# Products that nothing reads in thin half sub-steps of two attention passes, and new places for some VectorE work

## The reference, cut to what matters

```python
def _L1_attn_ref(x, Wq, Wk, Wv, Wo, bo):      # 16 heads of 16
    q, k, v = heads(x @ Wq), heads(x @ Wk), heads(x @ Wv)
    weights = softmax(q @ k.T / 4)
    return (weights @ v) @ Wo + bo
def _L1_ffn_ref(x, ...):                      # 8 experts of 32, the two best, low-rank part of 16
    w = top two of softmax(x @ G), zero elsewhere
    return sum_e w_e * down_e(silu(gate_e x) * up_e x) + sum_e w_e * B_e (A_e x)
x = layernorm(x + L1_attn(x)); x = layernorm(x + L1_ffn(x))
```

## Time and profile before

| | |
|---|---|
| median of 3 runs | 745.18 us |
| profiled execution: own time | 748.4 us |
| profiled execution: span of its instructions | 746.5 us |
| TensorE products busy | 702.6 us (94%) |
| VectorE, ScalarE, GpSimd busy | 508.2, 403.3, 106.0 us |
| first turned score of pass 0, 1, 2, 3 | 372.98, 449.69, 540.61, 624.46 us |

### The profile page before, as it was taken

The page is one execution under the profiler, slowest core; times in us unless marked ns, Lnnn a source line. Parts: engine busy times, 40 slices in busy tenths (PEclk is TensorE's granted clock), DMA queues, the critical chain, the costliest instruction groups (busy, mean ns, idle before and its releaser), DMA issues.

```text
span 746.5 us, 11415 instructions
## 1 busy us (share of the span) xinstructions
PE 702.6 (94%) x4044; PEld 483.4 (65%) x4044; DVE 508.2 (68%) x1158; ACT 403.3 (54%) x745; POOL 106.0 (14%) x116
## 2 busy tenths in 40 slices
PE   8999999999999999996799999999999999999975
PEld 5878987898779887895435533555564555445654
DVE  5667457755576666856877786779779787774353
ACT  5674347544665467452146754666547566476431
POOL 0202220232013331241201010200001000100010
PEclk9999999999999999998659985999999999899986
DMA  8300000010000010005505500152004500000000
GB/s 336 143 2 1 29 1 2 1 45 0 0 0 11 5 75 1 4 16 87 106 2 86 87 1 1 32 93 49 1 2 81 89 32 2 1 30 2 1 29 29
DMA packets 13997, 28.31 MB, mean 38 GB/s; under 512 B 2612, under 2 KB 3452, under 8 KB 13820
## 3 DMA queue, kind: packets, MB, share of 16 engines
q1 hardware_dynamic: 13948, 27.68, 15.9%
HBM read 12.60 MB, written 2.10 MB: 20 GB/s over the span
## 4 chain that ended last, share of the span: by engine, by line
PE 70%; DVE 15%; issue 7%; ACT 4%; DMA 2%; POOL 1%; SPq 0%; DVEq 0%; POOLq 0%; ACTq 0%
PE bank_y L414 11%; PE bank_q L355 10%; PE bank_st L1223 8%; DVE nmax L1865 7%; PE bank_c L1236 6%; PE bank_a L298 5%; PE side L1169 3%; PE bank_a L385 3%; PE side L1321 2%; PE side L1290 2%; PE bank_a L332 2%; PE bank_n L370 2%; PE bank_s L1200 2%; PE side L1183 2%; PE side L1256 2%
## 5 line engine op out<-in xcount | busy, mean ns | idle before, releaser
L1865 DVE TENSOR_REDUCE nmax<-bank_s 128x1 f32<-128x512 f32 x240 | 154.1, 683 | 68.5 <-PE bank_s L1200 67.3
L1580 ACT ACTIVATE shared<-bank_st 128x512 f32<-128x512 f32 x256 | 139.0, 596 | 69.2 <-PE bank_st L1223 68.1
L1200 PE MATMUL bank_s<-ks,qs 48*128 48x512 f32 x240 | 105.9, 504 | 8.9 <-DMA ks<-qk_lo 4.7
L1223 PE MATMUL bank_st<-qs,ks 50*128 50x512 f32 x256 | 105.5, 483 | 6.0 <-ACT shared L1580 4.4
L617 DVE SCALAR_TENSOR_TENSOR sq<-bank_q,bq,eq 128x512 f32<-128x512 f32 x64 | 47.6, 743 | 48.2 <-ACT eq L500 48.2
L1223 PEld LDWEIGHTS bank_st<-qs,ks 50*128 50x128 f32 x256 | 42.9, 197 | 54.3 <-issue 26.8
L1236 PE MATMUL bank_c<-shared,v 128*32 128x512 f32 x512 | 76.3, 671 | 0.0
L414 PE MATMUL bank_y<-m_hi,s_lo 128*128 128x256 f32 x256 | 73.2, 286 | 3.2 <-POOL s_lo L250 3.1
L414 PE MATMUL bank_y<-m_hi,s_hi 128*128 128x256 f32 x256 | 72.1, 282 | 0.0
L414 PE MATMUL bank_y<-m_lo,s_hi 128*128 128x256 f32 x256 | 72.1, 282 | 0.0
L250 POOL TENSOR_TENSOR s_lo<-sq,s_hi 128x512 fp32r<-128x512 f32 x32 | 42.8, 1336 | 186.2 <-ACT s_hi L505 186.2
(11 more groups left out here) (278 smaller groups left out, 1356.5 us busy)
## 6 DMA issues: line engine op xcount, KB each, us to landing
qs<-qk_hi SPq DMA_DIRECT2D x16, 256.0 KB, 4.8
ks<-qk_hi SPq DMA_DIRECT2D x16, 256.0 KB, 7.1
xT<-in_xT SPq DMA_DIRECT2D x4, 512.0 KB, 4.3
sq<-in_wqT SPq DMA_DIRECT2D x2, 1024.0 KB, 9.2
wo<-in_woT SPq DMA_DIRECT2D x1, 2048.0 KB, 13.1
xs<-in_x SPq DMA_DIRECT2D x1, 2048.0 KB, 18.0
qs<-qk_lo SPq DMA_DIRECT2D x8, 256.0 KB, 5.4
ks<-qk_lo SPq DMA_DIRECT2D x8, 256.0 KB, 7.6
```

The costliest lines, as they stand in the source:

```text
L1200: pe.matmul(score_bank(b, u)[:, :], qs[part, b % 2, slot, t * P:(t + 1) * P], ks[part, b % 2, slot, :], start=True, stop=True).then_inc(s_ ...
L1223: pe.matmul(bank_st[u % 2][:, :], ks[part, b % 2, slot, kt * P:(kt + 1) * P], qs[part, b % 2, slot, :], start=True, stop=True).then_inc(st ...
L1580: act.activation(probs[:, u % SLOTS, :], bank_st[u % 2][:, :], ACT.Exp, scale=SCALE1).then_inc(p_ready, 1)
L1865: dve.tensor_reduce(nmax[:, g, t, j:j + 1], score_bank(b, u)[:, :], AX.X, ALU.max, negate=True).then_inc(max_ready, 1)
```

## The change

It has four parts. (1) A function `keep_busy(home, count)` takes a bank and issues `count` products of 128x128 weights with 512 columns into it that nothing reads. It is called for bank_c ahead of pass 0 (3 products), and at the end of the half sub-steps n = 2, 3, 4, 5, 10, 11 (2 each) and 20 to 31 (1 each) of pass 0, and n = 0, 1, 6, 7, 8, 9, 12, 14, 15 (1 each) of pass 3, there for side bank n % 2: 36 products. (2) In pass 3, the last norm of batch 1 moves: its statistics from n = 5 and 6 to 9 and 13, the merge from 7 to 14, GpSimd's power behind that of batch 2, ScalarE's normalization from n = 9 and 10 to 15 and 16. (3) VectorE's scaling of the context goes ahead of `qk_rest` at n = 10, and behind `hidden` at n = 26. (4) VectorE's projections go ahead of the routing at n = 19 and 20.

```diff
@@ gpsimd body
-                if b > 1 and b + 1 == B:
-                    rstd(4, b - 2)
                 if b > 0:
                     rstd(3, b - 1)
                 if b + 1 < B:
                     keep_x2(b + 1)
-                if b > 1 and b + 1 < B:
+                if b > 1:
                     rstd(4, b - 2)
@@ tensor
+            def keep_busy(home, count):
+
+                take(home)
+                for _ in range(count):
+                    pe.matmul(banks[home][:, :], wqkv_hi[:, 0, 0:P], x2T_hi[:, 0, :], start=True, stop=True)
@@ tensor body, at the end of a half sub-step
                     if n == 27 and more:
                         turn_max(b + 1, 0)
+
+
+                    if b == 0 and n in (2, 3, 4, 5, 10, 11):
+                        keep_busy(n % 2, 2)
+                    if b == 0 and n >= 20:
+                        keep_busy(n % 2, 1)
+                    if not more and n in (0, 1, 6, 7, 8, 9, 12, 14, 15):
+                        keep_busy(n % 2, 1)
@@ tensor, ahead of the passes
             pe.wait_ge(first.res_ready, B)
+            keep_busy("c", 3)
             for b in range(B):
                 body(b)
@@ scalar last_half
-                if n in (9, 10):
-                    normalize(4, b - 2, x, (0, 1) if n == 9 else (2, 3))
+                if n in (15, 16):
+                    normalize(4, b - 2, x, (0, 1) if n == 15 else (2, 3))
@@ vector last_half
-                if n in (5, 6):
-                    expert_stats(b - 2, n - 5)
-                if n == 7:
+                if n in (9, 13):
+                    expert_stats(b - 2, n // 13)
+                if n == 14:
                     merge(4, b - 2)
@@ vector body
+                    if n in (10, 18):
+                        context_out(b, n // 8 - 1)
                     if n in (9, 10) and more:
                         qk_rest(b + 1, n - 9)
                     if n == 9:
                         split_maxima(b, 2)
-                    if n in (10, 18, 26):
-                        context_out(b, n // 8 - 1)
...
+                    if n in (19, 20) and most:
+                        projections(b + 2, n - 19)
                     if n == (17 if more else 16) and back:
                         route_scores(b - 1)
...
                     if n == (20 if more else 17) and back:
                         route_second(b - 1)
-                    if n in (19, 20) and most:
-                        projections(b + 2, n - 19)
                     if n in (e + 1, e + 3, e + 5, e + 7) and back:
                         weighted_up(b - 1, (n - e) // 2)
                     if n in (e + 2, e + 4, e + 6, e + 8) and back:
                         hidden(b - 1, (n - e) // 2 - 1)
+                    if n == 26:
+                        context_out(b, 2)
```

## The result

| | before | after |
|---|---|---|
| median | 745.22 us (13 runs beside those of after) | 741.54 us (13 runs) |
| ratio, 95% interval | | 0.9938 [0.991, 0.9965] |
| profiled execution: own time, span | 748.4, 746.5 us | 741.54, 739.7 us |
| mean granted clock in it | 0.941 | 0.958 |
| first turned score of pass 0, 1, 2, 3 | 372.98, 449.69, 540.61, 624.46 | 375.70, 452.70, 539.59, 623.46 |

What follows compares the result with a forecast made beforehand. In low-clock stretches TensorE, throttled for thin work, was taken to keep VectorE waiting. Terms -4.0 - 6.0 - 3.5 + 0.5 + 0.8 + 0.9 = -11.3 us took 748.4 to 737.1; as a median 734.0, range 728 to 741.

Steps and rivals of the forecast that it cites:

- start of pass 0, with n = 10, 11's products: Pass 0, n = 0 to 5: added products keep the clock up, gain 4.0 us; those at n = 10, 11 net nil.
- seam, with its products: End of pass 0 and start of pass 1: clock stays up, gain 6.0 us; twelve products cost 0.5.
- VectorE's and the other orders: Pass 3's moved norm of batch 1 gains 3.5 us; VectorE's other moves in passes 1 and 2 cost 0.9.
- pass 3's products: Nine products in pass 3, on TensorE's path at n = 0, 12 and 14, others in waits: cost 0.8 us.
- the 5.3: Start of pass 0: us that VectorE's maxima of 373 to 389.6 waited for scores, to fall to about 1.3.
- fourth rival: Products do not touch the clock: 749.6 us, chance 0.05; sign: n = 2's context still takes 1.9 us behind two products.
- first rival: Only part holds: clock falls at pass 1's n = 0 to 4, or pass 0's start despite three products; 738.5 us, chance 0.22.
- under the same chain: Pass 3, n = 5 to 16: the clock's part, at most 3.4 us, lies under the orders' chain; only 0.1 added.
- More comes: Falls at 536 and in pass 3's n = 28 do not return, products cost nothing: 729.3 us, chance 0.15.
- Falls only move: Other thin stretches drop instead (pass 2's n = 16 to 20, n = 8 to 12): 744 us, chance 0.08.
- Slower: The fourth rival: falls have another cause than thin work, products in low stretches are added time; +4.4 us, chance 0.05.

Runs made afterwards that it cites:

- e4: after without the three products ahead of pass 0 and the twelve at its n = 2 to 5, 10 and 11; median 741.31 us, ratio 0.9979.
- e5: after with only the twelve products of n = 20 to 31 of pass 0, all new orders kept; median 741.33 us, ratio 0.9934.
- e1: after with every added product left out, so the new orders alone; median 745.85 us, ratio 1.0029.
- e2: before with all 36 added products, in the old orders; median 747.0 us, ratio 1.003.
- e8: after with 128 instead of 512 columns in each of the 36 products; median 744.89 us, ratio 1.001.
- e9: after with 16 more products in TensorE's wait for a DMA ahead of the opening's first scores; median 740.94 us, ratio 0.9925.
- e3: after with each added product writing 32 instead of 128 output rows; median 737.59 us, ratio 0.9915.
- e15: e5 with the three products ahead of pass 0 and three at each of its n = 0 to 5; median 743.75 us, ratio 0.9963.
- e12: e5 with only the six products at odd n from 21 to 31 of pass 0; median 744.28 us, ratio 0.988.
- e13: before with only the moved norm of batch 1 in pass 3, no products; median 741.93 us, ratio 0.996.
- e14: before with only VectorE's moved scaling and projections, no products; median 748.34 us, ratio 1.0026.
- e11: e10 with added products of 32 output rows; median 738.36 us, ratio 0.989.
- e6: e4 with 32-row products, plus two behind each head's scores from h = 1 in the opening, one at pass 1's n = 2, 3; median 739.16 us, ratio 0.9879.
- e7: e6 with full products of 128 output rows in the same places; median 738.48 us, ratio 0.9895.
- e10: e7 without pass 3's products, plus e9's 16 in the DMA wait and one at each of pass 0's n = 0 to 5; median 741.89 us, ratio 0.9953.

## Why the prediction was wrong

The parts, forecast against measured: as differences of means, of medians, and of means without the longest executions.

| part | forecast | means | medians | without the longest | from |
|---|---|---|---|---|---|
| start of pass 0, with n = 10, 11's products | -4.0 | +0.4 | +0.2 | +0.4 | after less e4 |
| seam, with its products | -6.0 + 0.5 | -5.3 | -4.5 | -2.4 | e5 less e1 |
| VectorE's and the other orders | -3.5 + 0.9 | 0.0 | +0.3 | -1.8 | e1 less before |
| pass 3's products | +0.8 | +0.6 | 0.0 | +0.6 | e4 less e5 |
| sum, before rounding | -11.3 | -4.4 | -4.0 | -3.3 | after less before |

The first row holds in all three. How the rest is shared between the seam and the orders hangs on e1, of whose 12 executions five lie between 747.0 and 753.6 us: together the two stand firmly (-4.2 to -5.3), each alone does not.

**The start of pass 0 is the step that failed.** The prediction put it as "The three added products on bank c sit in the 1.39 us that TensorE idles before pass 0's first turned score, so they cost nothing, and are meant for the clock. If it then stays at 2.4 GHz, what stays of the 5.3". In the changed kernel's profile it never was at 2.4 GHz to stay there: 361 to 375.7 above is all at 0.50. I had read the row of 373 on, and of the opening only that it "is not touched". Once low, the products didn't lift it before n = 4. TensorE in n = 0, 2 and 3 of after:

```profile
376.85 2.07 PE L1155 MATMUL side<-down,hmT 72*128 72x256 f32 x4
...
383.16 1.93 PE L1240 MATMUL bank_c<-shared,v 128*32 128x512 f32 x8
385.02 1.22 PE L1113 MATMUL side<-x2T_hi,wqkv_hi 128*128 128x512 f32 x2
386.17 0.79 PE L1227 MATMUL bank_st<-qs,ks 50*128 50x512 f32 x1
```

The context of n = 2 still takes 1.93 us: that is the sign which the fourth rival named, and there its price came true, with two products at 1.15 us from start to start of the next pair (forecast 0.86) on a path where VectorE was waiting. n = 2 grew from 3.01 to 4.17 us, n = 3 from 1.48 to 2.30. At n = 4, at 390.8, it rose, too late. What level pass 0 finds differs from kernel to kernel in the profiles. Of the eight with no product there or in the opening, six were up from about 369 on and fell 0.7 to 1.0 us ahead of the first turned score, as before did, and two were low all along. Of the six with the three products, after, e2 and e8 were low all along, e9 fell 1.3 us ahead of it, and e3 and e15 were still up at it; e3 fell 2.5 us later, e15 did not. So the three products may hold a level that is up; they do not raise one that is down. And the prize was read from a single profile: five of those eight took 14.5 to 14.8 us for n = 0 to 5, not 16.64. So the second form of the first rival happened, the start falling in spite of the three products, and at its price: it was to give back 4 to 5 us, and the means say 4.4. Its 738.5 was still 3 us too low; by the means that is the orders, below. Where the start holds, as in e15, 2.8 of the 4.0 us came, with 18 products in the stretch.

**What made the level fall there.** The Trainium skill, page "TensorE: Matmul & The Clock Gate", section "Why this matters for your kernels", names idle gaps of TensorE between bursts of products as what drops the clock. The first fall bears it out: it comes in the 4.68 us wait for a DMA, and e9, which filled that wait, is without it. e9's fall of 356.9 may be of the same kind, for a wait of 1.69 us stands just ahead of it. For the others the page does not suffice: ahead of e9's of 445.6 TensorE was idle 0.55 us of 4.89, and ahead of the one at 696.5 in before not at all, in small products:

```profile
693.00:696.50 3.50, 3.50 (x24) 2.10 (x24) 0.71 (x5) 2.47 (x7) 0.00 (x0) 1.00 0.00 0
```

The fourth rival took the page as a reason that filling cannot help. In the DMA wait filling did remove the fall, and at the seam it helped where 0.52 us of the last 3.50 were idle, so it was no reason against either. Why a place falls in one execution and not in the next stays open.

**The seam: right in its mechanism.** The fall is gone in after, eight half sub-steps took 16.62 us against 23.37, and the maxima's idle time is 2.7 against 8.6. Its waits were sized by the like places at the end of pass 2, and that held. Two sizes were off, both to the dear side, so that the means still come near the forecast is in part luck. First, I had kept 0.7 back for a short fall in pass 1; after has one, and it costs more: 8.80 us for n = 4 where e1, at full clock, took 5.64. Second, the products. I took 0.23 us each from two like products on end, and hid most of it. Alone between two other kinds, also at full clock, one takes 0.43:

```profile
433.82 0.49 PE L1113 MATMUL side<-x2T_hi,wqkv_hi 128*128 128x512 f32 x1
434.25 0.50 PE L1227 MATMUL bank_st<-qs,ks 50*128 50x512 f32 x1
```

n = 20, 22 and 26 grew by 0.43, 0.42 and 0.51 us, the whole price, so VectorE's cover was not there; n = 21, 23 and 25 did not grow. The eight of n = 20 to 27 cost 1.14 us (14.65 to 15.79), against 0.5 forecast for twelve. The place of a product decides: e12's four in odd n cost 0.25.

**The orders: pass 3's chain holds, and the clock is not "under the same chain".** e13 and e1 show VectorE at n = 7 to 9 of pass 3, e13 first (its pass starts at 623.54), e1 below (620.06):

```profile
646.59 1.27 DVE L1863 TENSOR_REDUCE nmax<-bank_s 128x1 f32<-128x512 f32 x2
...
649.38 1.29 DVE L1863 TENSOR_REDUCE nmax<-bank_s 128x1 f32<-128x512 f32 x2 [0.90 <-PE bank_s L1198]
```

```profile
643.11 1.27 DVE L1871 TENSOR_REDUCE nmax<-bank_s 128x1 f32<-128x512 f32 x2
...
644.92 1.28 DVE L1871 TENSOR_REDUCE nmax<-bank_s 128x1 f32<-128x512 f32 x2
```

From the pass's start the first pair stands at 23.05 us in both, against 24.32 in before (648.78 less 624.46): 1.27 sooner, forecast 1.4. But in e13 the next pair waits 0.90 us for scores from a TensorE at half speed, and of n = 8 to 16 only 1.7 us are gained (21.80 against 23.46); e1, at full clock, gains 3.05 (20.41). So I was wrong to give the clock only 0.1 there: what the moved norm frees, a slow TensorE takes next. In after ScalarE did what was forecast, four normalizations in place of six:

```profile
650.24 2.07 ACT L1545 ACTIVATE xk<-xk,ln_shift,ln_rstd 128x256 f32<-128x256 f32 x4 [0.34 <-POOL ln_shift L1027]
```

Taken apart, the terms of the orders come out: the moved norm brought -2.9 in e13 (forecast -3.5), the other moves +1.4 in e14 (+0.9). That together, in e1, they bring nothing in the means (forecast -2.6) I can only bound. At equal clock, taking 0.32 us per us of low time, e1 is 1.3 us under before (0.0 and 0.32 x 4.2), and after 1.5 under e2 (4.1, less 0.32 x 8.0); e1 also has 4.2 us more of low time than before, and whether the orders cause that or 12 executions drew it stays open. The moves in passes 1 and 2 were mis-sized the other way: TensorE's turn of x3 at n = 11 does wait, as forecast, in pass 1

```profile
486.93 0.63 PE L1124 MATMUL side<-ident,xk 128*128 128x128 f32 x4 [0.48 <-DVE qk_lo L1870]
```

and n = 11 grew from 1.94 to 2.45 us, but n = 12 gave 0.34 of it back: 0.17 a pass where I took 0.45.

**The other rivals.** More comes: half true in this execution (n = 28 of pass 3 and n = 30 of pass 1 didn't fall), and over executions only chance, since e4, e5 and e9 to e11 have one or the other. Falls only move: in part. Products kept n = 8 to 11 of pass 3 high in all seven profiled kernels that had both them and the moved norm, and of the eight with the norm but without them only e1 had no fall there; but five of the first seven, after among them, fell at n = 16 (663.9 in after), and e4 less e5 is +0.6. Slower: no, but its mechanism, products at the lower level are added time, is what took the start.

**The faster versions.** e6 and e7 (ratios 0.9879 and 0.9895) and e11 (0.989) beat before by about 1.1%, e3 (0.9915) by 0.9%. Their means are 2.6 to 3.2 us under after's, some two or three times what such a difference stands to; the intervals of the ratios overlap with after's. All four have the seam's products. Opening products are in e6, e7 and e11, 32 rows in e3, e6 and e11. Rows of 32 took 3.2 us off after (e3) and 2.9 off e10 (e11), but 0.6 off e7 (e6); which of the two brings the gain stays open.

## What to carry to other kernels

Before a product is added to keep a clock up, look at the level that the stretch *starts* with, and where it first fell: a filler at the lower level is added time, and one ahead of the fall may save it. Look at more than one execution before you price the place, for the fall may not be there in the next. Price a filler between its real neighbours, not between its like, and put it where the other engine is late, not where it waits. When the clock of a kernel differs from execution to execution, compare means over many of them beside their granted clock, for two profiles differ by chance as much as by the change.

## What the runs showed of the hardware

- A product of 128 x 128 by 512 columns costs 0.23 us behind its like the earlier trace rows and 0.43 alone between a context and a score product, both at 2.4 GHz. With 32 rows of output in place of 128 it is 0.35: start to start 433.11 to 433.46 in e3.
- Products of 32 output rows left as little low time as those of 128: 53.5 and 60.6 us in e3 and after, 51.1 and 52.8 in e6 and e7, 49.3 and 58.6 in e11 and e10. Those of 128 columns left 79.0 (e8).
- The same program in the same place falls in one execution and not in the next: low time runs from 66 to 108 us in before, and each us of it is worth 0.32 us, not the 0.5 that a path of TensorE alone would give.
- Filling a wait of 4.7 us took away the fall in it (e9 to e11). The next came at 355.3 to 357.7, about where before has its second (358.6).
- The level also falls out of work without idle time: at 696.5 in before TensorE had been busy for all of the last 3.50 us.
